# The second attention product of layer 0 in one piece, between the two pairs of scores

## The reference, cut to what matters

```python
def _L0_attn_ref(x, Wq, bq, Wk, bk, Wv, bv, Wo, bo):     # 16 heads of 8 features
    q = (x @ Wq.T + bq).reshape(b, s, NHEADS, DK)
    k = (x @ Wk.T + bk).reshape(b, s, NHEADS, DK)
    v = (x @ Wv.T + bv).reshape(b, s, NHEADS, DV)
    w = jnp.einsum('bshd,bzhd->bhsz', q, k) / jnp.sqrt(jnp.float32(DV))
    w = jax.nn.softmax(w, axis=-1)
    vw = jnp.einsum('bhsz,bzhd->bshd', w, v).reshape(b, s, NHEADS * DV)
    return vw @ Wo.T + bo
# layer 0: x = x + ga * attention(h), with 2048 x 2048 scores for each of 16 heads, then a
# mixture of 16 experts with one expert a token and a shared part;
# layer 1: causal attention of 8 heads with shared keys and values, then a gated mixing layer.
```

## Time and profile before

| what | value |
|---|---|
| median of 3 runs | 1083.95 us |
| profiled execution | 1085.42 us |
| its span | 1083.6 us |
| TensorE busy | 1007.7 us (93%) |
| VectorE busy | 900.6 us (83%) |
| ScalarE busy | 824.1 us (76%) |
| granted TensorE clock, mean | 0.972 |

### The profile page before, as it was taken

How to read it: one execution, slowest core, us unless ns; L and a number is a source line. 1 busy time by engine, 2 the same in 40 slices (tenths; PEclk the granted TensorE clock), 3 DMA queues, 4 the chain that set the end, 5 groups by cost and what they waited for, 6 DMA issues and landing times.

```text
span 1083.6 us, 22172 instructions
## 1 busy us (share of the span) xinstructions
PE 1007.7 (93%) x8654; PEld 341.6 (32%) x8654; DVE 900.6 (83%) x1153; ACT 824.1 (76%) x1584; POOL 195.8 (18%) x370
## 2 busy tenths in 40 slices
PE   6889999999999999999998899999989998899997
PEld 2422222222222222222232244334344563323323
DVE  8989999999999999999988677766778767897604
ACT  4149999998999998999986577666755676656785
POOL 4533200003000003000024200231042113110112
PEclk9569999999999999999999899999999999999997
DMA  3820511000000000000001441115200431200000
GB/s 98 204 79 7 141 32 26 6 2 2 2 2 2 3 2 2 2 1 3 2 2 31 144 129 51 40 32 94 35 2 9 141 106 37 34 10 1 1 11 11
DMA packets 46422, 41.68 MB, mean 38 GB/s; under 512 B 5598, under 2 KB 44478, under 8 KB 46318
## 3 DMA queue, kind: packets, MB, share of 16 engines
q1 hardware_dynamic: 44062, 34.87, 13.1%
q0 software_dynamic: 1824, 5.25, 1.7%
q10 hardware_dynamic: 432, 0.13, 0.0%
HBM read 26.44 MB, written 13.30 MB: 37 GB/s over the span
## 4 chain that ended last, share of the span: by engine, by line
PE 71%; DVE 13%; ACT 8%; issue 4%; DMA 1%; POOL 1%; another core or an unknown queue 1%; SPq 0%; POOLq 0%; ACTq 0%; DVEq 0%
PE O L989 26%; PE T L957 14%; PE S L917 9%; DVE mx L1280 8%; ACT PT L1527 4%; PE S L924 4%; PE T L966 3%; PE S L1102 2%; PE S L1068 1%; ACT PT L1521 1%; PE S L1058 1%; PE T L1110 1%; PE S L966 1%; PE T L998 1%; PE T L1090 1%
## 5 line engine op out<-in xcount | busy, mean ns | idle before, releaser
L1280 DVE TENSOR_REDUCE mx<-S 128x2 f32<-128x1024 f32 (+2 forms) x672 | 759.3, 1180 | 72.4 <-PE S L917 25.3
L1527 ACT ACTIVATE PT<-T 128x512 f32<-128x512 f32 (+2 forms) x1280 | 675.8, 580 | 116.5 <-PE T L966 49.4
L989 PE MATMUL O<-PT,Va 128*9 128x256 f32 (+1 forms) x4032 | 317.7, 387 | 3.3 <-ACT Os L1562 3.3
L917 PE MATMUL S<-Ks,Qs 48*128 48x512 bf16 x1024 | 205.5, 394 | 12.1 <-DVE mx L1280 9.6
L957 PE MATMUL T<-Qs,Ks 51*128 51x512 bf16 x1024 | 202.0, 387 | 13.4 <-ACT PT L1527 9.3
L957 PEld LDWEIGHTS T<-Qs,Ks 51*128 51x128 bf16 x1024 | 56.2, 93 | 224.1 <-issue 126.7
L989 PEld LDWEIGHTS O<-PT,Va 128*9 128x9 f32 x4032 | 59.8, 88 | 207.1 <-issue 197.5
L924 PE MATMUL S<-K,Qs 96*128 96x512 bf16 (+3 forms) x320 | 89.4, 349 | 5.3 <-DVE mx L1280 4.9
L966 PE MATMUL T<-Qs,K 99*128 99x512 bf16 (+3 forms) x256 | 67.4, 344 | 11.9 <-ACT PT L1527 8.3
L989 PE MATMUL O<-PT,V 128*17 128x512 f32 (+3 forms) x616 | 72.5, 540 | 0.0
L917 PEld LDWEIGHTS S<-Ks,Qs 48*128 48x128 bf16 x1024 | 52.4, 95 | 34.7 <-DVE mx L1280 27.3
(11 more groups left out here) (303 smaller groups left out, 815.3 us busy)
## 6 DMA issues: line engine op xcount, KB each, us to landing
Qs<-in_L_ffn_experts SPq DMA_DIRECT2D x28, 192.0 KB, 2.4
Ks<-in_L_ffn_experts SPq DMA_DIRECT2D x20, 192.0 KB, 2.6
Vf<-sorted_x SPq DMA_DIRECT2D x12, 256.0 KB, 4.8
sorted_y<-Vf SPq DMA_DIRECT2D x12, 256.0 KB, 2.3
Qs<-rows_q SPq DMA_DIRECT2D x24, 128.0 KB, 4.5
rows_q<-q SPq DMA_DIRECT2D x7, 384.0 KB, 2.5
Qs<-rows_q SPq DMA_DIRECT2D x36, 64.0 KB
sorted_x<-XP POOLq DMA_DIRECT2D x1, 1792.0 KB, 10.7
```

The costliest lines, as they stand in the source:

```text
L917: m = e.matmul(two[:, i, :], Qs[r0:r0 + 48, hp, q0:q0 + 128], Ks[r0:r0 + 48, hp, CH * kb:CH * kb + CH], start=True, stop=True, tile_positi ...
L989: m = e.matmul(acc[32 * g:32 * g + d1, lo:hi], v, PT[(2 * j + g // 2) % 4][:, p0 + lo:p0 + hi], start=fresh, stop=True, skip_group_check=n ...
L1280: e.tensor_reduce(mx[:, u % 2, h0:h0 + 2, kb], two[:, :, 0:n], AX.X, ALU.max).then_inc(free, 1)
L1527: e.activation(PT[(2 * j + pair) % 4][:, CH * i + lo:CH * i + CH], bank[:, lo:CH], ACT.Exp).then_inc(free, 1)
```

## The change

In units 0 to 11 of layer 0, the second product of the step before is emitted whole between the two pairs of T; nothing is emitted behind the second pair's S. From unit 12 on the order is as before.

```diff
         if L == 0 and k:
+
+            halves = ((0, 1), ()) if u < 12 else ((0,), (1,))
             emit_s()
-            emit_pv(J - LAG, (0,))
+            emit_pv(J - LAG, halves[0])
             do_light(0.5)
             do_later()
             emit_st(J, 1)
             for _ in range(k - 1):
                 emit_s()
-            emit_pv(J - LAG, (1,))
+            if halves[1]:
+                emit_pv(J - LAG, halves[1])
```

## The result

| | median | runs | ratio to before |
|---|---|---|---|
| before | 1083.37 us | 4 (1082.62 to 1086.41) | |
| after | 1155.74 us | 4 (1152.39 to 1156.77) | 1.0655, 95% interval 1.0637 to 1.0673 |

The change makes the kernel 72.4 us slower; 1153 was forecast. The profiled execution took 1156.77, 71.35 more than that of before (1085.42), and its span is 1155.0.

The account below looks back on a forecast made before the run. VectorE's pace of 2.26 us a step was taken as the bound. 191 steps at +0.39 give +74.5, less 3.1 and 2.4 for pieces, so +69: 1154.5 profiled, 1153 as median, range 1136 to 1166.

Parts of the forecast that it names:

- the gap g: Least spacing of two T pairs when TensorE waits idle for the exponential: taken as 1.14 us, bounds 1.10 and 1.18.
- All marks named for it: Signs expected in the profile after, up to unit 11: two alternating T spacings, 1.1 to 1.2 and about 1.5 us.
- The sum: Units 0 to 11: 74.5 for the steps, -3.1 and -2.4 for pieces within units, together +69 us.
- The step before: One step of the kernel before, in the changed stage: 2.26 us, said to be VectorE's pace.
- The sentence that the waits did no harm: Kernel before, steady state: T's waits for the exponential do no harm because the pairs are evenly spaced.
- the 70.3 us of the earlier trace: Kernel before: total wait for the exponential of 160 weight loads of T, read as T's steady-state wait.
- The extra pieces: Output copy wait, output transpose and turn of the maxima, per unit: 1.18 us against 1.44, over 12 units -3.1.
- The block of four pieces: Further pieces in two units, put at 3.3 us together, becoming about 2.1 as partly hidden: -2.4 in all.
- Rival 1: T follows a whole product at 0.86 instead of 0.97 us: step 2.54, total 1132; chance 0.07.
- Rivals 2 and 3: Rival 2: TensorE's work decides, 1070 us. Rival 3: VectorE's pace hides the wait, 1084. Chance 0.02 each.
- Rival 4: TensorE, idling some 0.6 of 2.65 us, is granted a lower clock: step 4.4, total 1478 us; chance 0.02.

Follow-up runs that it names:

- behind: Changed kernel with the whole product of units 0 to 11 behind the second pair's S instead of between the pairs: 1159.28 us, ratio 1.0674.
- two_between: Changed kernel with two half products, one behind the other, between the two pairs in units 0 to 11: 1161.07 us, ratio 1.0697.
- half_dose: The change made in units 0 to 5 alone, the later units as in the kernel before: 1119.72 us, ratio 1.0319.
- short_exp: Changed kernel with exponentials of units 0 to 11 (but for two steps) over 256 of 512 columns: 1111.53 us, ratio 1.0244.
- s_behind: Changed kernel with both S tiles behind the second pair in units 0 to 11, the product still between the pairs: 1136.14 us, ratio 1.0459.
- short_max_after: Changed kernel with every row maximum of layer 0 over half of the keys: 1149.09 us, ratio 1.0585.
- split_wait_after: Changed kernel with a T pair's two bank waits taken apart in layer 0, the first matmul waiting for its own bank only: 1137.31 us, ratio 1.0476.
- short_max_before: Kernel before with every row maximum of layer 0 over half of the keys: 1077.55 us, ratio 0.9925.
- split_wait_before: Kernel before with a T pair's two bank waits taken apart in layer 0, the first matmul waiting for its own bank only: 1077.15 us, ratio 0.9932.
- product_256: Changed kernel with 256 instead of 512 columns in each whole product of units 0 to 11: 1101.99 us, ratio 1.0177.
- short_product: Changed kernel with 64 instead of 512 columns in each whole product of units 0 to 11: 1162.18 us, ratio 1.0709.

## Why the prediction was right

**The mechanism.** A pair of T waits for the exponential of the previous pair's first tile, so two pairs can't be closer than the gap g; the whole product widens the other gap beyond g, and what it saves goes into a wait. All marks named for it came: two spacings in turn, idle time on the exponential ahead of every first pair, T 0.97 to 0.98 behind the product, copies 44.06 apart (43.5 forecast), VectorE 87% busy, the clock at 0.99, later units within 3 us. `behind`, `two_between` and `half_dose` show that the place between the pairs, the width of the matmuls and the start are not the cause; `short_exp` moves g alone and the time with it; `s_behind` moves work from the long gap into the short one and wins. `short_max_after` clears VectorE. `split_wait_after` shows that the wait is for the later of a pair's two banks. A fourth bank for T, which would take the wait away, was not tried.

**Sizes.** The sum, term by term:
- g: 1.16, not 1.14. The one bare pair in the trace had it; I averaged it with a spacing of 1.12 from the steady state. With 0.01 more for the product the step is 2.68, not 2.65.
- The step before: 2.256, as forecast, but not for the forecast's reason. I read it as VectorE's pace because (3.48 - 1.22)/2 gave it. `short_max_before` shows the same 2.256 with VectorE relieved: it is one spacing of 1.09, TensorE's own work, and one of 1.16 to 1.17. The sum needed only the number, so that it came out right here is luck. The sentence that the waits did no harm was wrong; `split_wait_before` gains 6.5 us by shortening them. Nor do the 70.3 us of the earlier trace rows show T waiting: TensorE's matmuls stood idle for the exponential for 1.8 us there. The steps give 191 x (2.683 - 2.256) = 81.6, not 74.5.
- The extra pieces: 44.06 - 16 x 2.683 = 1.13 a unit, against 37.60 - 16 x 2.256 = 1.50: 12 x -0.37 = -4.4, not -3.1.
- The block of four pieces: (46.67 - 44.06) against (43.06 - 37.60) = 2.61 against 5.46, twice -2.85, so -5.7 and not -2.4. I had put 3.3 for the 5.46 that my own rows gave, and more of it fell into the idle time than I took.
- Together 81.6 - 4.4 - 5.7 = 71.5, against 71.35 measured. In this sum the first unit and unit 11 are taken as the others; by the copies they lost 7.9 and 7.3, not 6.5, and about as much (2.7) came back behind unit 11. That this evens out is chance, too.

The larger term and the larger discounts nearly cancelled: 69 was closer than its parts.

**Rival 1** did not come true: T stands 0.98 behind the product's start (336.43 to 337.41), not 0.86. The Trainium skill, page "TensorE: Matmul & The Clock Gate", section "Part 2: What happens when you issue a matmul", has weights loaded ahead only under conditions. Whether these hold between product and T no run here shows; the trace has T's weights loaded at 337.41, no earlier than T itself. **Rivals 2 and 3** needed g below 0.75; it is 1.16. **Rival 4**, the clock, did not occur in the changed kernel (0.99), but it was nearer than the chance of 0.02 said: the changed kernel began the stage at the lower level and left it some 8 us later than the kernel before. With 0.43 of some 2.05 us of TensorE's work in a step gone (`product_256`) it left it only at about 110 us, and with less still (`short_product`) not for good until the stage was nearly over.

## What to carry to other kernels

When a stage waits for banks in turn, look at the spacing of the instructions that take them, not only at the work in a round: with too few banks a round costs the sum of max(gap's work, bank's turnaround) over its gaps, so work spread evenly beats less work in one lump. Here the turnaround was 1.16. The rule gives the changed kernel, `behind` and `short_exp` within 0.01 us a step; for the kernel before and `product_256` it gives 2.32 where 2.26 was measured, since work of 1.09 in a gap was not stretched to 1.16. Read the turnaround where nothing else stands between two takers. And when an engine's pace equals the step, relieve that engine once before you call it the bound; two bounds here differed by less than 0.01 us. Idle time before weight loads is not idle time of the engine: look at the matmuls' own.

## What the runs showed of the hardware that I had not expected

- The cost of going from the product (four column strips) to T is paid at the change: 0.98 for 16 records of 256 columns as for 8 of 512, and 0.55 for 8 of 256; the turn of the maxima follows a whole product after 0.87 (331.80 to 332.67 in `behind`), and T then 0.32 behind that.

```profile
331.80 1.05 PE L993 MATMUL O<-PT,Va 128*9 128x512 f32 x8
332.67 0.39 PE L941 MATMUL T<-idb,n 128*12 128x128 bf16 x4
332.99 0.39 PE L961 MATMUL T<-Qs,Ks 51*128 51x512 bf16 x2
```

- A pair that waits idle for two banks starts about 0.08 later than a matmul that waits for one (1.16 against 1.08, `split_wait_after`); taking the waits apart gave 0.7% in layer 0.
- The clock can stay at its lower level for nearly a whole stage. With the product cut to 64 columns it was granted 0.50 before the stage and 0.51 in it, for 525 us, with TensorE 88% busy by the trace. The changed kernel, 80% busy and with 0.56 us of idle time in each 2.68, rose to the upper level and kept it (0.99).
